# One recurrence, two forms: an element-by-element state scan replaced by masked pair products over levels of a 128-token tile

## The reference

```python
def step(state, inp):
    rt, kt, vt, wt = inp
    kv = kt[..., :, None] * vt[..., None, :]
    out = jnp.einsum('bhk,bhkv->bhv', rt, state + u[None, :, :, None] * kv)
    return (state * wt[..., None] + kv, out)
...
_, outs = jax.lax.scan(step, init, xs)
```

## Time and profile before

| | |
|---|---|
| median of 3 runs | 8584.15 us (8583.95 to 8587.62) |
| the profiled execution: its own time | 8596.22 us |
| the profiled execution: its span | 8594.4 us |
| first scan of the trace (L1078) starts at | 3604.9 us |
| last scan of the trace starts at | 5207.2 us |
| busy: PE, DVE, ACT, POOL | 6067.9, 5534.0, 3038.5, 2830.0 us |

### The profile page before, as it was taken

How to read it: one execution, slowest core, us unless ns; L and a number is a source line. 1 busy time by engine, 2 the same in 40 slices (tenths; PEclk the granted TensorE clock), 3 DMA queues, 4 the chain that set the end, 5 groups by cost and what they waited for, 6 DMA issues and landing times. The chain is left out here.

```text
span 8594.4 us, 84244 instructions
## 1 busy us (share of the span) xinstructions
PE 6067.9 (71%) x22816; PEld 3551.2 (41%) x22816; DVE 5534.0 (64%) x10124; ACT 3038.5 (35%) x6978; POOL 2830.0 (33%) x2050
## 2 busy tenths in 40 slices
PE   3686877868678686677766775677777775887554
PEld 1453544535455354122212221244555443665332
DVE  6775766757577575599848996477878776121334
ACT  1563655636456364100020001133333322333333
POOL 0452534525355252244413441044444442000000
PEclk6897989979899898699969997755555555555777
DMA  0000000000000000000000000000000000000000
GB/s 11 17 1 14 1 1 14 1 14 1 2 13 1 14 1 6 1 0 0 0 5 0 0 0 0 14 1 0 0 0 0 0 1 4 0 0 8 3 3 8
DMA packets 3953, 34.57 MB, mean 4 GB/s; under 512 B 401, under 2 KB 785, under 8 KB 2065
## 3 DMA queue, kind: packets, MB, share of 16 engines
q1 hardware_dynamic: 3600, 30.63, 1.0%
HBM read 29.58 MB, written 1.05 MB: 4 GB/s over the span
## 5 line engine op out<-in xcount | busy, mean ns | idle before, releaser
L744 POOL TENSOR_TENSOR slabs<-slabs 128x512 f32<-128x512 f32 x768 | 1034.7, 1377 | 1546.2 <-DVE slabs L680 1546.2
L1078 DVE TENSOR_TENSOR_SCAN slabs<-slabs 128x512 f32<-128x512 f32 x512 | 884.9, 1728 | 124.6 <-POOL slabs L1094 111.1
L1359 DVE MAX8 slabs<-slabs 128x8 f32<-128x512 f32 x1152 | 740.5, 687 | 295.1 <-ACT slabs L1310 285.3
L1094 POOL TENSOR_TENSOR slabs<-slabs 128x512 f32<-128x512 f32 x512 | 648.2, 1266 | 742.9 <-PE psum L1035 476.6
L1035 PE MATMUL psum<-slabs 128*128 128x512 f32 x1024 | 578.1, 646 | 296.5 <-POOL slabs L1094 296.5
L1393 POOL TENSOR_SCALAR slabs<-slabs 128x512 f32<-128x512 f32 x256 | 399.6, 1561 | 1043.0 <-DVE slabs L1366 1043.0
L629 ACT ACTIVATE slabs<-slabs 128x96 f32<-128x96 f32 x1536 | 553.0, 361 | 387.6 <-DVE slabs L709 387.6
L1275 PEld LDWEIGHTS psum<-slabs 128*128 128x128 f32 x3072 | 677.4, 333 | 7.5 <-ACT slabs L1301 7.5
L1275 PE MATMUL psum<-slabs 128*128 128x9 f32 (+1 forms) x3072 | 663.0, 359 | 0.0
L1261 PE MATMUL psum<-slabs 8*128 8x512 f32 (+1 forms) x768 | 596.9, 1136 | 79.7 <-DVE slabs L1342 58.5
L1269 PE MATMUL psum<-constants,slabs 128*128 128x128 f32 x1536 | 419.1, 433 | 274.3 <-POOL slabs L1397 263.7
(11 more groups left out here) (332 smaller groups left out, 11270.6 us busy)
## 6 DMA issues: line engine op xcount, KB each, us to landing
slabs<-F SPq DMA_DIRECT2D x6, 2756.5 KB, 10.2
weights<-S SPq DMA_DIRECT2D x4, 645.0 KB, 3.8
weights<-M SPq DMA_DIRECT2D x1, 2184.0 KB, 9.1
weights<-R SPq DMA_DIRECT2D x2, 1079.5 KB, 5.0
slabs<-x SPq DMA_DIRECT2D x1, 1024.0 KB, 4.8
slabs<-falloff SPq DMA_DIRECT2D x1, 1024.0 KB, 4.7
out<-slabs SPq DMA_DIRECT2D x1, 1024.0 KB, 3.9
weights<-L SPq DMA_DIRECT2D x1, 840.0 KB, 4.5
```

Of the source, the lines that this page charges most:

```text
L744: nc.gpsimd.tensor_tensor(out[:, at, :], normed[:, at, :], table, ALU.mult).then_inc(rope_done, 1)
L1078: nc.vector.tensor_tensor_scan(state[b % 2][:, 1:SEQ + 1], decay[:, cols(b)], fed[b % 2], 0.0, ALU.mult, ALU.add).then_inc(state_ready, 1)
L1094: nc.gpsimd.tensor_tensor(read[b % 2], r[:, cols(b)], state[b % 2][:, 0:SEQ], ALU.mult).then_inc(read_ready, 1)
L1359: nc.vector.max(eight, wk if k else s).then_inc(top_step, 1)
```

## The change

The loop over value features goes, and with it `spread`, `pick`, `gather` and the phase that loaded the table. In its place `pairwise_scan` builds, for each sequence, tile of 128 tokens (4 per sequence) and head, the 128 x 128 matrix of pair weights between tokens j (on partitions) and i, and multiplies it by the values.

- The sum over features between tokens is a matmul over the 64 rows of a head. The decays between j and i are put into `k` and `r` themselves, level by level (`LEVELS`): at level `size` the tile is cut into blocks of that many tokens, paired two by two, and the product is right for the pairs with j in the earlier and i in the later block of a couple. Then `r` of each later block is multiplied by the whole decay of the block before it (DVE, L1106), and `k` of each earlier block by that of the block behind it (POOL, L1135), which makes both right for the next level. Level 0 is the token with itself, with `bonus` for `k`.
- A job is a level and a sequence: 32 jobs. PE makes its 8 products (L1052) into one of three pairs of PSUM banks. At levels 1, 2, 4 and 8 DVE places them by a mask with `copy_predicated` (L1100), at levels 16, 32 and 64 ACT copies the blocks (L1147).
- The decays of whole blocks come from seven products of neighbours (DVE, L1088).
- Between tiles a state is passed on: the keys are transposed (L1060), multiplied by the values (L1065), and DVE links the states of the tiles (L1115, L1118). The output is pair weights times values plus state times `r` (L1076, L1079).
- So the values are needed with tokens on the partitions: for f == 2 the projection in `token_mix` is four matmuls of 128 tokens each (L928) in place of one of 512. ACT makes `bonus` there (one more instruction for each sequence).
- The masks are loaded once (256 KB), beside the copy that opens the network.

```diff
-HD_R = 64
...
-    with phase(nc, "copied") as (block, copied):
+    with phase(nc, "copied masks_loaded") as (block, copied, masks_loaded):
+        @block.sync
+        def _(sp):
+            sp.dma_start(m.weights[:, LEVEL_MASKS:LEVEL_MASKS + P * len(MASKED_LEVELS)], ins["levels"]).then_inc(masks_loaded, 16)
+            sp.wait_ge(masks_loaded, 16)
...
-        state_scan(nc, m, w, ins, decay, k, v, r, out)
+        pairwise_scan(nc, m, w, decay, k, m.slab(8), v, r, out)
...
-    xxx = m.slab(8)
+    xxx = bonus = m.slab(8)
...
+                elif f == 2:
+                    for t in range(SEQ // P):
+                        at = slice(b * SEQ + t * P, b * SEQ + t * P + P)
+                        last = nc.tensor.matmul(ps[:, 4 + n % 4, t * P:t * P + P], mixed[0][:, at], w("Wv"), start=True, stop=True)
+                    last.then_inc(projected, 1)
+                    return
                 else:
-                    out, weight = ps[:, 4 + n % 4, :], w(["Wk", "Wv", "Wr", "Wg"][f - 1])
+                    out, weight = ps[:, 4 + n % 4, :], w(["Wk", None, "Wr", "Wg"][f - 1])
...
+                if f == 1:
+                    nc.scalar.activation(bonus[:, cols(b)], ps[:, 4 + n % 4, :], ACT.Copy, scale=w("time_first"))
...
-def state_scan(nc, m, w, ins, decay, k, v, r, out):
+LEVELS = [0, 1, 2, 4, 8, 16, 32, 64]
+MASKED_LEVELS = [1, 2, 4, 8]
+LEVEL_MASKS = 2304
+def pairwise_scan(nc, m, w, decay, k, bonus, v, r, out):
     ps = m.psum
...
+    tiles = SEQ // P
+    keysT = m.slab(6).rearrange("p (b t d) -> p b t d", b=BATCH, t=tiles)
+    states = m.slab(7).rearrange("p (b t d) -> p b t d", b=BATCH, t=tiles)
+    pairs = [m.slab(16 + b // 2)[:, 1024 * (b % 2):1024 * (b % 2) + 1024].rearrange("p (u i) -> p u i", i=P) for b in range(BATCH)]
+    whole = {1: decay}
+    at = 0
+    for size in LEVELS[2:] + [P]:
+        whole[size] = m.slab(15)[:, at:at + TOK // size]
+        at += TOK // size
+    masks = {size: m.weights[:, LEVEL_MASKS + P * n:LEVEL_MASKS + P * n + P] for n, size in enumerate(MASKED_LEVELS)}
+    jobs = [(level, b) for level in range(len(LEVELS)) for b in range(BATCH)]
+    by_vector = BATCH * (1 + len(MASKED_LEVELS))
+    updates = len(LEVELS) - 1
+
+    def blocks(a, size, b):
+        per = a.shape[-1] // BATCH
+        return a[:, b * per:b * per + per].rearrange("p (n s m) -> p n s m", s=2, m=size)
+
+    with phase(nc, "whole_step pair_product masked placed r_decayed k_decayed cleared keysT_product keysT_copied "
+                   "fed_product state_step out_product") as (
+            block, whole_step, pair_product, masked, placed, r_decayed, k_decayed, cleared, keysT_product, keysT_copied,
+            fed_product, state_step, out_product):
+        @block.tensor
+        def _(pe):
+            for n, (level, b) in enumerate(jobs):
+                if level >= 2:
+                    pe.wait_ge(r_decayed, BATCH * (level - 2) + b + 1)
+                    pe.wait_ge(k_decayed, BATCH * (level - 2) + b + 1)
+                if 3 <= n < by_vector + 3:
+                    pe.wait_ge(masked, n - 2)
+                elif n >= by_vector + 3:
+                    pe.wait_ge(placed, n - by_vector - 2)
+                source = bonus if level == 0 else k
+                for t in range(tiles):
+                    tokens = slice(b * SEQ + t * P, b * SEQ + t * P + P)
+                    for h in range(2):
+                        rows = slice(64 * h, 64 * h + 64)
+                        last = nc.tensor.matmul(ps[:, 2 * (n % 3) + h, t * P:t * P + P], source[rows, tokens], r[rows, tokens],
+                                                start=True, stop=True)
+                last.then_inc(pair_product, 1)
+
+            pe.wait_ge(placed, len(jobs) - by_vector)
+            for b in range(BATCH):
+                pe.wait_ge(k_decayed, BATCH * (updates - 1) + b + 1)
+                for t in range(tiles - 1):
+                    last = nc.tensor.transpose(ps[:, b, t * P:t * P + P], k[:, b * SEQ + t * P:b * SEQ + t * P + P], m.ident)
+                last.then_inc(keysT_product, 1)
+            for b in range(BATCH):
+                pe.wait_ge(keysT_copied, b + 1)
+                for t in range(tiles - 1):
+                    last = nc.tensor.matmul(ps[:, 4 + b, t * P:t * P + P], keysT[:, b, t, :], v[:, b * SEQ + t * P:b * SEQ + t * P + P],
+                                            start=True, stop=True)
+                last.then_inc(fed_product, 1)
+            for b in range(BATCH):
+                pe.wait_ge(r_decayed, BATCH * (updates - 1) + b + 1)
+                for t in range(tiles):
+                    tokens = slice(b * SEQ + t * P, b * SEQ + t * P + P)
+                    if t:
+                        pe.wait_ge(state_step, 2 * BATCH * (t - 1) + 2 * b + 2)
+                    for h in range(2):
+                        rows, own = slice(64 * h, 64 * h + 64), slice(b * SEQ + t * P + 64 * h, b * SEQ + t * P + 64 * h + 64)
+                        last = nc.tensor.matmul(ps[rows, b, t * P:t * P + P], v[:, own], pairs[b][:, tiles * h + t, :],
+                                                start=True, stop=(t == 0))
+                        if t:
+                            last = nc.tensor.matmul(ps[rows, b, t * P:t * P + P], states[:, b, t, rows], r[:, tokens],
+                                                    start=False, stop=True)
+                last.then_inc(out_product, 1)
+
+        @block.vector
+        def _(dve):
+            link = Chain(dve, whole_step)
+            for size in LEVELS[1:]:
+                sides = whole[size].rearrange("p (n s) -> p n s", s=2)
+                link(nc.vector.tensor_tensor(whole[2 * size], sides[:, :, 0], sides[:, :, 1], ALU.mult))
+            for n, (level, b) in enumerate(jobs):
+                dve.wait_ge(pair_product, n + 1)
+                seen = ps[:, 2 * (n % 3):2 * (n % 3) + 2, :].rearrange("p h (t i) -> p (h t) i", i=P)
+                size = LEVELS[level]
+                if level == 0:
+                    diagonal = m.ident.rearrange("p (o i) -> p o i", o=1).broadcast_to([P, 2 * tiles, P])
+                    nc.vector.tensor_tensor(pairs[b], seen, diagonal, ALU.mult).then_inc(masked, 1)
+                    continue
+                if n < by_vector:
+                    mask = masks[size].bitcast(mybir.dt.int32).rearrange("p (o i) -> p o i", o=1).broadcast_to([P, 2 * tiles, P])
+                    dve.wait_ge(masked, n - BATCH + 1)
+                    nc.vector.copy_predicated(pairs[b], mask, seen).then_inc(masked, 1)
+                late = blocks(r, size, b)[:, :, 1, :]
+                before = blocks(whole[size], 1, b)[:, :, 0, :]
+                dve.wait_ge(whole_step, updates)
+                if level >= 2:
+                    dve.wait_ge(r_decayed, BATCH * (level - 2) + b + 1)
+                nc.vector.tensor_tensor(late, late, before.broadcast_to(late.shape), ALU.mult).then_inc(r_decayed, 1)
+            for t in range(tiles - 1):
+                for b in range(BATCH):
+                    dve.wait_ge(fed_product, b + 1)
+                    dve.wait_ge(cleared, 1)
+                    for h in range(2):
+                        rows, own = slice(64 * h, 64 * h + 64), slice(t * P + 64 * h, t * P + 64 * h + 64)
+                        after = states[rows, b, t + 1, 64 * h:64 * h + 64]
+                        if t == 0:
+                            nc.vector.tensor_copy(after, ps[rows, 4 + b, own]).then_inc(state_step, 1)
+                        else:
+                            dve.wait_ge(state_step, 2 * BATCH * (t - 1) + 2 * b + h + 1)
+                            nc.vector.scalar_tensor_tensor(out=after, in0=states[rows, b, t, 64 * h:64 * h + 64],
+                                                           scalar=whole[P][rows, tiles * b + t:tiles * b + t + 1],
+                                                           in1=ps[rows, 4 + b, own], op0=ALU.mult, op1=ALU.add).then_inc(state_step, 1)
+
+        @block.gpsimd
+        def _(pool):
+            nc.gpsimd.memset(m.slab(7), 0.0).then_inc(cleared, 1)
+            for n, (level, b) in enumerate(jobs):
+                if level == 0:
+                    continue
+                size = LEVELS[level]
+                early = blocks(k, size, b)[:, :, 0, :]
+                behind = blocks(whole[size], 1, b)[:, :, 1, :]
+                pool.wait_ge(pair_product, n + 1)
+                pool.wait_ge(whole_step, updates)
+                if level >= 2:
+                    pool.wait_ge(k_decayed, BATCH * (level - 2) + b + 1)
+                nc.gpsimd.tensor_tensor(early, early, behind.broadcast_to(early.shape), ALU.mult).then_inc(k_decayed, 1)
+
         @block.scalar
         def _(act):
...
+            for n, (level, b) in enumerate(jobs):
+                if n < by_vector:
+                    continue
+                size = LEVELS[level]
+                act.wait_ge(pair_product, n + 1)
```

(21 more changed lines are left out.)

93 lines of the change are left out of this document (1 added, 92 removed).

## The result

The changed kernel takes **7317.26 us** (median of 4 runs, 7315.03 to 7320.36) against 8585.89 us for the one before: a ratio of 0.8521 (95% interval 0.8508 to 0.8535), 1268.6 us less. The profiled execution took 7317.57 us.

What follows compares the result with a forecast made beforehand. The prediction took the loop as a chain of DVE work slowed by POOL: 8596.22 − 1364.4 (both old stretches) + 144.4 (two new ones of 72.2) + 3.0 (masks) = 7379.2, less 12.07 for the median, 7367 us; range 7335 to 7450.

Steps and rivals of the forecast that it cites:

- The rest of the program only shifts: Code outside the replaced stretches: the change is worth what its own stretches get shorter, nothing else gains or loses.
- the prediction's own lower bounds: Masked jobs at 1.5, levels 16 to 64 at PE's 0.9, output halves side by side: 12 us a layer less, 7343 us.
- Items 1 and 2: Entry and exit of the stretch, 2.8 us a layer; block products and level 0 on DVE, 8.1 us.
- Item 3: Levels 1 to 8, sixteen masked jobs paced by DVE: 1.75 us a job, 28.0 us a layer.
- the dearer bound of 2.3: Masked copy from PSUM at two cycles an element: 2.3 us, or 1.1 us more a job.
- the addition of 0.25 a job for POOL: Masked jobs: POOL's update of k meets DVE's update in a part of the jobs, 0.25 us added to 1.5.
- Item 4: Levels 16 to 64, twelve jobs: POOL's 0.73 and DVE's 0.43 one after the other, 1.15 a job, 13.8 us a layer.
- Item 5: The tail from the last update of k through states and output products to the last eviction: 19.5 us a layer.
- The estimate from the Trainium skill's "TensorEngine Tiling", Overview: Output products in the tail: up to twofold speed for a stationary side of at most 64 columns, tail 5.1 us shorter.
- Item 6: Outside the phase: value projections and the copy for `bonus` cost zero, loading the masks once 3 us.
- The rival on rows and a low clock: Halves of 64 rows do not overlap and TensorE stays at 1.2 GHz: 68 us more a layer, 7504 us; chance 0.10.
- The rival on a start for each run of elements: POOL's strided updates pay a start for each of 2032 runs a layer; at 0.40 us each, 8953 us; chance 0.01.

Runs made afterwards that it cites:

- the two padded kernels: Waits that are met at once added to VectorE's stream ahead of the recurrence: 86 instructions in the kernel before, 8574.54 us; 42 in the changed kernel, 7347.80 us.
- no_k_update: Changed kernel with POOL's 28 updates of k a layer cut to a single element each; 7307.99 us.
- same_cols: Changed kernel with the output products of both heads written to PSUM partitions 0 to 63; 7325.35 us.
- same_rows: Changed kernel with the pair products of both heads reading rows 0 to 63; 7446.45 us.
- half_products: Changed kernel with the masked copy only over later blocks' columns and pair products of levels 1 to 64 on 64 columns for 128; 7336.66 us.
- late_compact: Changed kernel with the masked copy only over later blocks' columns and both heads' states side by side in 64 columns, pair products whole; 7325.99 us.
- compact_first: late_first with both heads' states side by side in 64 columns, output products from states on 64 rows; 7306.43 us, ratio 0.8507.
- late_first: Changed kernel with the masked copy only over later blocks' columns and all output products that need no state issued first; 7293.79 us, ratio 0.8497.

## Why the prediction was wrong

By its own steps:

- **"The rest of the program only shifts"** is the step that failed. It put a term at nothing without a row for it. Some 26 us were gained elsewhere, 20.6 of them in the attention of block 2, where the two padded kernels show that the loop's place in VectorE's stream decides over 22 to 26 us. With the stretches as measured and this step right, the time would have been 7367 − 2 × 11.7 − 1.6 = 7342, inside the range. The 25 us that the stretches and the masks came out too high (items 3 to 6) would not have left the range alone either; it took both. But those 11.7 a layer lie within the 12 that the prediction's own lower bounds allowed, and for the rest of the program it allowed nothing. Of the some 6 us left no run tells the cause; the two traces differ by 5.6 us in one stage with the granted clock.
- **Items 1 and 2** held: 2.7 and 8.0 us for 2.8 and 8.1, with L1095 at 1.22 us and seven products in 3.43.
- **Item 3** was 1.8 us too high a layer. The copy costs 1.29 us, near L680's 1.22 and far from the dearer bound of 2.3; a job without POOL takes 1.51 (no_k_update), as summed. Mis-sized was the addition of 0.25 a job for POOL: it came to 1.9 us for sixteen, 0.12 a job. In three of the first seven jobs POOL's update starts 0.07 to 0.17 us ahead of VectorE's, which then takes 0.95 for 0.40 us. From the eighth on the two start within 0.03 us of each other, VectorE keeps its 0.40, and POOL takes 0.92 to 0.96 us for 0.67, which nobody waits for. The lock that the Trainium skill ("SBUF — State Buffer", who interferes with whom) describes agrees with this: where the two meet, one of them is held up. But few meetings went against VectorE. The estimate made with that page, 0.73 us in every job, would have been 11.7 us a layer, where 1.9 were lost.
- **Item 4** was 4.3 us too high. I set 1.15 for POOL and VectorE one after the other. But POOL's update takes 0.83 to 0.87 us there (one of 1.60 at the start apart) for 0.67 alone, so VectorE's 0.42 holds it up by 0.2 us only, and TensorE's 0.89 (predicted 0.9) sets the pace, just above POOL.
- **Item 5** was 5.4 us too high: I took the records at 0.11 us, and same_cols shows that they are 0.055 because the column halves overlap. The estimate from the Trainium skill's "TensorEngine Tiling", Overview, 5.1 less a layer, was closer than the sum. The chain of states cost 4.96, not 3.5.
- **Item 6**: the masks cost 1.4 us, not 3. Projection and `bonus` show nothing, as said.
- **The rival on rows and a low clock** got 0.10 and did not come, but same_rows shows what it would have cost: +68 us a layer, as the prediction said.
- **The rival on a start for each run of elements** did not come either: L1135 takes 0.84 to 0.98 us at level 1, with 256 runs of one element, and 0.85 at level 64, with four runs.

## What to carry to other kernels

Price TensorE's work in records of one shape, with what stands beside it: halves of rows or columns that alternate cost half, a product of 64 columns cost what one of 128 did and the clock too, and a change between 128 and 64 rows costs 0.25 us, so group products by shape and put those that need no late input first. Before an untouched stage is called constant, look in the trace for idle time put down to issue in its loops: code that grows ahead of them can remove or bring 20 us. And time a masked or strided form at its shortest run before halving its elements.

## What the runs showed of the hardware

- `copy_predicated` from PSUM with 1024 fp32 elements in a row: 1.29 us; with 512 in runs of 1 or 2: 1.31; in runs of 4 or 8: 0.70.
- The same products in the same number were granted 0.50 up to level 64 with both heads in one half of the rows, TensorE busy all the time, and 1.00 from the end of level 0 on with the heads in either half. From 1.00 it fell back when products of 64 columns followed, and in some tails after a wait of 1.83 us, while in others it stayed.
- An fp32 product of 64 by 128 with 128 columns, two records, costs 0.11 us at the upper clock with its neighbour in the other rows, 0.21 at the lower, and 0.43 alone at the lower (same_rows). With 64 columns it costs the same, at either clock (half_products). One of 128 by 64 costs 0.11 us with its neighbour in the other columns and 0.22 alone (same_cols), both at the upper clock.
- A change between a product on 128 rows and one on 64 rows: 0.25 us (late_compact); grouped, either costs some 0.12 (compact_first, late_first).
- A loop of VectorE lost 1.6 to 2.2 us in each of 12 gaps, or nothing, by 86 or 42 instructions more ahead of it; each gap has a packet of the fetch queue beside it.
